# Five edits to a macaron block (mixture of experts, selective scan, mixture of experts) on one core

## The reference

```
def ffn(h):                       # mixture of 8 experts, top 1, and a shared expert
    logits = h @ router_w         # 256 -> 8
    e = argmax(logits); score = sigmoid(max(logits))
    out = silu(xs @ gate_w[e]) * (xs @ up_w[e]) @ down_w[e],  xs = h * score
    return out + silu(h @ sh_gate) * (h @ sh_up) @ sh_down
def ssm(h):                       # selective scan over the 512 tokens, 16 states
    dt_x, B, C = split(h @ W_x.T, [64, 16, 16])
    dt = softplus(dt_x @ W_dt.T + b_dt)
    state = exp(dt * A) * state + dt * B * h
    return sum_n(state * C) + h * D
x = x + 0.5 * ffn(layernorm(x))
x = x + ssm(layernorm(x))
x = x + 0.5 * ffn(layernorm(x))
```

## Time and profile before

| what | us |
|---|---|
| three runs | 507.39, 507.84, 508.14 (median 507.84) |
| the profiled execution, span from first to last instruction | 512.9 |
| busy: PE, DVE, ACT, POOL in that span | 438.5, 342.4, 260.3, 292.6 |

### The profile page before, as it was taken

The page is one execution under the profiler, slowest core; times in us unless marked ns, Lnnn a source line. Parts: engine busy times, 40 slices in busy tenths (PEclk is TensorE's granted clock), DMA queues, the critical chain, the costliest instruction groups (busy, mean ns, idle before and its releaser), DMA issues. The chain is left out here.

```text
span 512.9 us, 7182 instructions
## 1 busy us (share of the span) xinstructions
PE 438.5 (85%) x2264; PEld 309.2 (60%) x2264; DVE 342.4 (67%) x552; ACT 260.3 (51%) x499; POOL 292.6 (57%) x226
## 2 busy tenths in 40 slices
PE   5988899999779597659868886877999999999995
PEld 5855455555334465558767666766984656555553
DVE  5557333333386666988899989999996593333332
ACT  1210233332116669986999999997851111333331
POOL 4302366663324137698799879986891005776463
PEclk9869999999977899989979997998999999999999
DMA  8943122210312012214213331232220298333221
GB/s 286 385 154 92 35 63 65 63 59 32 125 39 64 1 61 65 83 42 105 84 61 97 87 89 63 100 100 69 85 81 1 73 328 280 97 112 103 63 61 39
DMA packets 37667, 49.90 MB, mean 97 GB/s; under 512 B 5498, under 2 KB 26814, under 8 KB 37632
## 3 DMA queue, kind: packets, MB, share of 16 engines
q1 hardware_dynamic: 32368, 38.91, 24.2%
q0 software_dynamic: 5264, 10.54, 7.0%
HBM read 37.33 MB, written 16.70 MB: 105 GB/s over the span
## 5 line engine op out<-in xcount | busy, mean ns | idle before, releaser
L408 POOL TENSOR_TENSOR gs<-hs,c_sb 128x1024 f32<-128x1024 f32 x63 | 148.3, 2370 | 53.0 <-DVE hs L1126 35.5
L1126 DVE TENSOR_TENSOR_SCAN hs<-da,bank 128x1024 f32<-128x1024 f32 x64 | 145.1, 2278 | 9.8 <-PE bank L796 9.7
L796 PE MATMUL bank<-ident,dbx_t 128*128 128x128 f32 x512 | 73.7, 290 | 35.5 <-DVE hs L1126 29.3
L697 PE MATMUL bank<-w_gu,tt 128*128 x184 | 91.1, 617 | 4.1 <-ACT tt L467 4.1
L796 PEld LDWEIGHTS bank<-ident,dbx_t 128*128 128x128 f32 x512 | 60.6, 149 | 50.3 <-DVE hs L1126 39.1
L509 ACT ACTIVATE da<-dt_sb,a_neg 128x511 f32<-128x511 f32 x128 | 84.9, 713 | 7.7 <-DVE hs L1126 7.7
L363 POOL DMA_INDIRECT da<-rows,row_token x46 | 47.2, 1026 | 70.7 <-DVE row_token L1021 57.2
L523 ACT ACTIVATE dbx_t<-dtx_t,h_sb 128x256 f32<-128x256 f32 x194 | 83.8, 497 | 2.7 <-PE bank L796 2.7
L1034 DVE SCALAR_TENSOR_TENSOR q_sb<-th,bank 128x256 f32<-128x256 f32 x46 | 19.4, 421 | 90.2 <-ACT th L462 90.2
L812 PE MATMUL bank<-ident,gs 128*128 128x128 f32 x504 | 71.6, 290 | 8.7 <-POOL gs L408 8.6
L462 ACT ACTIVATE th<-bank,da 128x256 f32<-128x256 f32 x46 | 21.8, 473 | 99.2 <-PE bank L697 99.2
(11 more groups left out here) (125 smaller groups left out, 529.9 us busy)
## 6 DMA issues: line engine op xcount, KB each, us to landing
c_sb<-c_dram SPq DMA_DIRECT2D x64, 256.0 KB, 3.1
rows<-xn_no SPq DMA_DIRECT2D x12, 516.0 KB, 6.5
x_sb<-in_x SPq DMA_DIRECT2D x4, 512.0 KB, 5.8
w_gu<-in_gate_w SPq DMA_DIRECT2D x2, 1024.0 KB, 10.1
w_gu<-in_up_w SPq DMA_DIRECT2D x2, 1024.0 KB, 11.1
w_dn<-in_down_w SPq DMA_DIRECT2D x2, 1024.0 KB, 10.7
xn_no<-token_out SPq DMA_DIRECT2D x4, 512.0 KB, 5.5
rest<-x_sb SPq DMA_DIRECT2D x4, 512.0 KB, 4.9
```

The costliest lines, as they stand in the source:

```text
L408: nc.gpsimd.tensor_tensor(gs[:, s % 2], hs[:, s % RING], c_sb[:, s % RING].unsqueeze(1).to_broadcast([P, KC, L]), ALU.mult).then_inc(sc_g, 1)
L697: last = nc.tensor.matmul(H[j % 2][:, :], tt[:, j % 2, 2 + k], w_gu[:, k, bass.ds(e, 1), :].squeeze(1), start=(k == 0), stop=(k == KC - 1))
L796: mm = nc.tensor.transpose(DBX[s % 2][:, k, i * P:(i + 1) * P], dbx_t[:, s % TURNS, i, k * P:(k + 1) * P], ident[:])
L1126: nc.vector.tensor_tensor_scan(hs[:, s % RING].rearrange(flat), da[:, s % RING].rearrange(flat), DBX[s % 2][:, :, :].rearrange(flat), 0.0, ...
```

## The change

1. **Router in column groups.** w_rt is padded to 32 columns and becomes the stationary operand; the four sequences' 512 tokens stream, and sequence b's logits land in PSUM partitions 32b to 32b+31 of one bank. ACT copies the bank, PE turns it back in four transposes (`route_turn`). The routers leave the scan of the last sequence. Run 0's router moves behind all the layer norm transposes, with both halves of the first shared batch ahead of it.
2. **Reordered transition**, and parts of the lists around it: the shared expert's steps, `normalise(1,1)` behind the softplus, the copies of xnT, `skip` from n=3 to n=6, the memset of the gather slots from between the layer norm's steps to POOL's start.
3. **B's columns behind the transposes**: `project_bt` in the scan comes after `turn_dbx`.
4. **Row table stored once**: one table of rows of 2x258 words; the first seven tiles of run 1 are gathered as half rows, with indices 2t and 2t+1.
5. **Softplus bias in the product**: w_dt has a 65th row, b_dt, and the projection's output has a row of ones there (ACT Identity with a column of the identity matrix as bias). w_x is padded to 128 columns. The relu becomes a max inside a DVE instruction.

```diff
-            def route(r, b):
-                c = 2 * r
-                if r == 1:
-                    pe.wait_ge(sc_dve, states_by("dve", min(N * (BATCH - 1) + (ROUTES + (N,))[b] + 3, STATES)))
-                pe.wait_ge(ln_xnT, (GT // 2) * c + 2 * b + 2)
-                for i in range(LT * b, LT * (b + 1)):
-                    for k in range(KC):
-                        last = nc.tensor.matmul(LG[r][:, i, :], xnT[:, k, i * P:(i + 1) * P], w_rt[:, k, :],
+            def route(r):
+                pe.wait_ge(ln_xnT, (GT // 2) * (2 * r + 1))
+                for k in range(KC):
+                    for b in range(BATCH):
+                        last = nc.tensor.matmul(LG_T[32 * b:32 * (b + 1), :], w_rt[:, k, :], xnT[:, k, b * L:(b + 1) * L],
                                                 start=(k == 0), stop=(k == KC - 1))
+                last.then_inc(rt_lg, 1)
+
+            def route_turn(r):
+                pe.wait_ge(rt_lgc, r + 1)
+                for i in range(LT):
+                    last = nc.tensor.transpose(Y[:, i * P:(i + 1) * P], lg_sb[:, i * P:(i + 1) * P], ident[:])
                 last.then_inc(rt_logits, 1)
...
                 for b in range(BATCH):
-                    sp.dma_start(row_tiles[0][:, rows_of(b), :], xn_no[:, rows_of(b), :]).then_inc(xn_out, 16)
-                for b in range(BATCH if r == 1 else 0):
-                    sp.dma_start(row_tiles[1][:, rows_of(b), 0:D + 2], xn_no[:, rows_of(b), :]).then_inc(rows_full, 16)
+                    sp.dma_start(row_tiles[r][:, rows_of(b), 0:D + 2], xn_no[:, rows_of(b), :]).then_inc(xn_out, 16)
...
             xn_rows(0)
+            sp.wait_ge(ff_out[0], 16 * 2)
+            sp.dma_start(row_tiles[1][:, :, D + 2:], xn_no[:]).then_inc(table_set, 16)
+            sp.wait_ge(table_set, 16)
...
             def project_abs(b, k):
                 act.wait_ge(pj_z, KC * b + k + 1)
-                nc.scalar.activation(w_exp[:, k], pj_bank(b, k), ACT.Abs, bias=b_sb[:, k:k + 1]).then_inc(pj_abs, 1)
-                nc.scalar.activation(dt_sb[:, k, seq(b)], pj_bank(b, k), ACT.Relu, bias=b_sb[:, k:k + 1]).then_inc(pj_max, 1)
+                nc.scalar.activation(w_exp[:, k], pj_bank(b, k), ACT.Abs).then_inc(pj_abs, 1)
+                act.wait_ge(pj_abs, KC * b + k + 1)
+                nc.scalar.activation(w_exp[:, k], w_exp[:, k], ACT.Exp, scale=-1.0).then_inc(pj_exp, 1)
+
+            def project_u(b, k):
+                act.wait_ge(pj_exp, KC * b + k + 1)
+                nc.scalar.activation(dt_sb[:, k, seq(b)], w_exp[:, k], ACT.Copy, bias=1.0).then_inc(pj_u, 1)
...
             def project_w(b, k):
-                nc.vector.tensor_scalar(pj_bank(b, k), w_exp[:, k], 1.0, -1.0, ALU.add, ALU.add).then_inc(pj_w, 1)
-                nc.vector.tensor_tensor(pj_bank(b, k), w_exp[:, k], pj_bank(b, k), ALU.subtract).then_inc(pj_rest, 1)
+                dt = dt_sb[:, k, seq(b)]
+                if b == 0:
+                    nc.vector.tensor_scalar(dt, w_exp[:, k], 1.0, None, ALU.add).then_inc(pj_u, 1)
+                nc.vector.scalar_tensor_tensor(out=dt, in0=dt, scalar=-1.0, in1=w_exp[:, k],
+                                               op0=ALU.add, op1=ALU.subtract).then_inc(pj_rest, 1)
+                nc.vector.scalar_tensor_tensor(out=dt, in0=pj_bank(b, k), scalar=0.0, in1=dt,
+                                               op0=ALU.max, op1=ALU.subtract).then_inc(pj_max, 1)
             def project_dt(b, k):
-                nc.vector.tensor_tensor(pj_bank(b, k), log_w[:, k], pj_bank(b, k), ALU.add).then_inc(pj_sum, 1)
-                nc.vector.tensor_tensor(dt_sb[:, k, seq(b)], pj_bank(b, k), dt_sb[:, k, seq(b)], ALU.add).then_inc(pj_dt, 1)
+                nc.vector.tensor_tensor(dt_sb[:, k, seq(b)], log_w[:, k], dt_sb[:, k, seq(b)],
+                                        ALU.add).then_inc(pj_dt, 1 if b == 0 else KC)
...
             # PE, scan(b), state n
-                    if more and n == 4:
-                        project_bt(b + 1)
-                    if not more and n in ROUTES:
-                        route(1, ROUTES.index(n))
                     if s + 2 < STATES:
                         turn_dbx(s + 2)
+                    if more and n == 4:
+                        project_bt(b + 1)
...
-                    if more and n in (late, late + 1):
-                        project_z(b + 1, n - late)
-                    if n == 3:
+                    for k in range(KC):
+                        if more and n == ((0, 4), (1, 4))[b == 0][k]:
+                            project_z(b + 1, k)
+                    if n == 6:
                         skip(b)
...
             # PE, run 0
-                    shared_gate_up(0, 0, 0)
-                if b > 0:
-                    route(0, b - 1)
-            route(0, BATCH - 1)
+                if b in (1, 2):
+                    shared_gate_up(0, 0, b - 1)
+            route(0)
+            route_turn(0)
+            shared_gate_up(0, 1, 0, (0,))
             count(0)
-            shared_gate_up(0, 0, 1)
-            shared_gate_up(0, 1, 0)
+            shared_gate_up(0, 1, 0, (1,))
             shared_down(0, 0)
+            shared_gate_up(0, 1, 1)
             sequence(0)
-            shared_gate_up(0, 1, 1)
             shared_down(0, 1)
             routed(0)
             for fo in range(KC):
                 shared_gate_up(0, 2, fo)
+            shared_gate_up(0, 3, 0)
             shared_down(0, 2)
...
             project_bt(0)
-            for fo in range(KC):
-                shared_gate_up(0, 3, fo)
-            ln_transposes(1, 2)
+            shared_gate_up(0, 3, 1)
             for h in range(2):
                 turn_dt(0, h)
+            ln_transposes(1, 2)
+            turn_dbx(0)
             ln_transposes(1, 3)
-            turn_dbx(0)
+            turn_dbx(1)
             ln_transposes(1, 4)
-            turn_dbx(1)
             shared_down(0, 3, (0,))
...
             # PE, before run 1
             ln_transposes(2, 7)
+            shared_gate_up(1, 1, 1)
+            route(1)
             shared_down(1, 0, (1,))
-            route(1, BATCH - 1)
-            shared_gate_up(1, 1, 1)
+            route_turn(1)
             count(1)
             shared_gate_up(1, 2, 0)
```

More of the change, by code:

```diff
@@ L182, in macaron_kernel @@
         ln_stats, ln_rstd, ln_xn, ln_tp, ln_xnT = (sem(f"ln_{s}") for s in ("stats", "rstd", "xn", "tp", "xnT"))
-        rt_logits, rt_top, rt_exp, rt_onehot, rt_count, rt_read, rt_expert, rt_score, rt_place, rt_seq, rt_ids = (
-            sem(f"rt_{s}") for s in ("logits", "top", "exp", "onehot", "count", "read", "expert", "score", "place", "seq",
-                                     "ids"))
+        rt_lg, rt_lgc, rt_logits, rt_top, rt_exp, rt_onehot, rt_count, rt_read, rt_expert, rt_score, rt_place, rt_seq, rt_ids = (
+            sem(f"rt_{s}") for s in ("lg", "lgc", "logits", "top", "exp", "onehot", "count", "read", "expert", "score", "place",
+                                     "seq", "ids"))
         sh_gu, sh_tanh, sh_mul, sh_hidden, sh_y, sh_x = (
@@ L200, in macaron_kernel @@
         a_ready = sem("a_ready")
-        pj_all, pj_copy, pj_bt, pj_btc, pj_z, pj_abs, pj_max, pj_exp, pj_w, pj_rest, pj_ln, pj_sum, pj_dt, pj_tp, pj_dtx = (
-            sem(f"pj_{s}") for s in ("all", "copy", "bt", "btc", "z", "abs", "max", "exp", "w", "rest", "ln", "sum", "dt", "tp",
-                                     "dtx"))
+        pj_all, pj_copy, pj_bt, pj_btc, pj_z, pj_abs, pj_exp, pj_u, pj_rest, pj_max, pj_ln, pj_dt, pj_tp, pj_dtx = (
+            sem(f"pj_{s}") for s in ("all", "copy", "bt", "btc", "z", "abs", "exp", "u", "rest", "max", "ln", "dt", "tp", "dtx"))
+        w_pad = sem("w_pad")
         c_rows = sem("c_rows")
@@ L359, in experts, with gather @@
                 rows_back = (token_out, out_flat)[r]
-                def gather(j, lo, hi, source, done):
+                def gather(j, lo, hi, source, done, row):
                     u = j % XR
@@ L374, in experts @@
                 for j in range(XR):
-                    gather(j, 0, WIDE[0], rows[0], ff_in)
+                    gather(j, 0, WIDE[0], (rows[0], half_rows)[r], ff_in, (row_token[:, j:j + 1], row_half[:, 0, j:j + 1])[r])
                 if r == 1:
@@ L386, in experts @@
                     if j + XR < NR:
-                        gather(j + XR, 0, WIDE[r], rows[r], ff_in)
+                        gather(j + XR, 0, WIDE[r], rows[r], ff_in, row_token[:, j + XR:j + XR + 1])
                     if r == 1 and j in DRAINS:
@@ L572, in _ @@
                 project_abs(0, k)
-            project_exp(0)
             project_ln(0)
-            for fo in range(KC):
-                shared_tanh(0, 3, fo)
-            ln_copies(1, 1)
+            shared_tanh(0, 3, 1)
             act.wait_ge(a_ready, 2)
-            ahead(0)
-            ln_copy(1, 4)
+            act.wait_ge(pj_dt, KC)
+            decay(0)
+            ln_copy(1, 2)
+            outer(0)
+            ln_copy(1, 3)
```

(31 more changed lines are left out.)

191 lines of the change are left out of this document (102 added, 89 removed).

## The result

The changed kernel takes 518.75 us (median of 6 runs, 517.09 to 521.19), the kernel before 507.99 (6 runs beside it, 506.08 to 519.68): 1.0223 times as long, 95% interval 1.0188 to 1.0257. The forecast was 495.8, 490 to 504. An execution of the kernel before takes either 501 to 511 us or, with a lower granted clock of TensorE, 514 to 520; the ratios go by the shorter ones alone and the medians by all, and since the one whose rows stand above (span 512.9, clock 0.943) is of the longer kind, a second profile of the same kernel, `before_again` (span 504.6, clock 0.963), is what the changed kernel is measured against here.

A forecast was written before the change was run, and what follows sets the result against it. No single engine bounds the kernel: PE's routed loops and shared expert and DVE's scan follow one another. 4.1 + 7.5 + 1.5 + 2.3 + 1.0 - 4.4 = 12.0 us off 507.84 gives 495.8, range 490 to 504.

The forecast's parts named there:

- Router: Column-group router products on PE: only neighbouring products overlap, because each is a pair of records on the same columns; 3.9 us.
- full overlap: Rival for the router: all four column groups run side by side, 1.7 us, 2.2 better per run, 491.4 in all; chance 0.17.
- Routing of run 0: Way to the first routed tile: earlier rows and shorter router bring it forward; gain 4.1 us, from 2.3 to 5.8.
- The part put down to the memset: Run 0's routing: moving the gather-slot memset off DVE's normalise (4.05 us, elsewhere 1.4) makes the last rows ready 2.7 earlier.
- Transition: Stretch from run 0's routed loop to the scan, reordered; gain 7.5 us, 4 to 10.
- the gain is the clock: Transition: PE idles less, so `project` and `project_z` take 1.7 us each instead of 3.73 and 3.8.
- Scan: The four sequences: gains of 1.5 us in the first, 2.3 in the second and third, 1.0 in the last.
- 8 steps of 0.66 become 4 of 0.7 and one of 1.1: Softplus on DVE in the scan: fewer steps plus a joined addition save 1.4 us a sequence.
- late z less: First scan sequence: one late z fewer, counted within its 1.5 us gain without a size of its own.
- skip and a router leave n=4: Last sequence: without skip (1.8 us) and router (1.7) there, PE starts the next gate and up earlier; gain 1.0 us.
- Way to run 1: Scan's end to run 1's first tile: longer router, four transposes and PE's 1.7 us wait ahead of `count`; loss 4.4, 2.2 to 7.4.
- ACT paces: Rival for the scan: ACT's lead is used up, 2.3 us lost and 0.5 extra paid three times, 499.6; chance 0.09.

The follow-up runs named there:

- before_memset: The kernel before with only GpSimd's memset of the row buffers moved ahead of its rstd work; 506.74 us, ratio 1.002 to the kernel before.
- hidden_first: old_scan with the second gate product of the third shared batch put ahead of combine(0) in VectorE's transition list; 504.72 us, ratio 0.9939 to the kernel before.
- scratch_sbuf: old_scan with the softplus scratch of the second to fourth sequence in SBUF instead of a PSUM bank; 526.1 us, ratio 1.0391 to the kernel before.
- turns_back: skip3 with the turns of dt at steps 8 and 10 again instead of 9 and 11; 509.08 us, ratio 1.0082 to the kernel before.
- skip3: The changed kernel with the skip products at step 3 of each sequence again instead of step 6; 512.93 us, ratio 1.0138 to the kernel before.
- old_scan: The changed kernel with every edit of the scan's lists undone (softplus, skip, B's columns, turns of dt); 505.51 us, ratio 0.9968 to the kernel before.
- best3_warm: old_scan plus hidden_first's exchange, a GpSimd wait, run 1's router earlier, and a last-batch gate and up made twice in the transition; 500.61 us, ratio 0.9913.
- after_warm: The changed kernel with the last shared batch's second-half gate and up products made twice in the transition; 529.18 us, ratio 1.0225 to the kernel before.

## Why the prediction was wrong, step by step

*Router.* 3.9 us forecast, 1.92 measured: the full overlap that was a rival, as the Trainium skill, "TensorEngine Tiling (Array Packing)", Theoretical Speedup, has it with its up to 4x. That pairs of records on the same columns forbid it was wrong.

*Routing of run 0.* 4.1 us earlier forecast, 4.07 against the same profile, 5.7 against before_again. Idle stretch (4.75) and cold down (5.38) came as forecast. The part put down to the memset isn't one by itself (before_memset).

*Transition.* 7.5 us forecast, -0.9 measured (35.62 to 36.54 us from the first gate product to scan 0). The step that failed is "the gain is the clock": 3.73 against 1.7 was read from an execution that fell to half clock there; before_again has 1.96. Against the profile that the forecast was read from, the same stretch is 5.1 us shorter (41.68 to 36.54), inside its 4 to 10. The reordering itself made the transposes late: the down product ahead of them starts 12.4 us behind the first gate product (9.2 in before_again), with a third half ahead of it and its hidden half behind `combine`, and is slow in both (5.4 us); hidden_first gives 2.0 back.

*Scan, the step that decides.* "8 steps of 0.66 become 4 of 0.7 and one of 1.1" and "late z less", 1.5 + 2.3 + 1.0 us to gain; 13.1 lost. (The 1.5 doesn't come out of its terms either: 1.4 less the net 1.2 leaves 0.2, and the late z has no price.) Three things stand in their place. First, three of the new form's five steps work in SBUF alone, where GpSimd's products block them: 2.35 instead of 1.1 and 0.91 instead of 0.69; scratch_sbuf shows the mechanism by itself. VectorE's busy time in the first three sequences, forecast 4.2 lower, is 1.1 higher. Second, moved steps wait for other engines: 3.4 for u at n=3, of which the forecast had seen 1.2, and 5.2 for the turn of dt at n=11, whose queue neighbour, the addition, was not followed to GpSimd's normalise (turns_back takes these waits away and is 2.8 us shorter by the ratios). VectorE's idle time in the first three sequences grows by 7.6. Third, "skip and a router leave n=4" was counted as a gain; without them a second GpSimd product stands beside VectorE's normalise, and skip at 6 meets TensorE at half clock (0.50): 4.4 us in the last sequence (skip3). The parts overlap: undone alone, softplus gives 9.3 and skip 4.3 by the ratios, together with B's columns 12.9. The softplus's part is by the windows more waits than form, but no run takes the form back alone; turns_back to old_scan, some 1.1% by their ratios, is the form, its places and B's columns.

*Way to run 1.* -4.4 forecast with a router of 3.9, so -2.4 with the measured one; -2.6 measured. Right, and PE's wait ahead of `count` is the 1.7 forecast, answering:
```profile
402.66 1.92 PE L647 MATMUL bank<-xnT,w_rt 128*32 128x512 f32 x16
...
408.62 0.23 PE L660 MATMUL bank<-onehot,before 128*128 128x128 bf16 x1 [1.68 <-DVE onehot L986]
```

*ACT paces, memory, routed loops.* Not seen: ACT is busy 184.0 us of the scan, 183.0 before, and the loops moved by 0.5 and 0.4 us.

The sum was also carried from one long execution to a median of short ones unscaled. The range left 0.07 for the other side and described it by the router's clock alone; no case had the scan's engines blocking each other, though one row of a VectorE step at 4.05 us beside a GpSimd memset was on the table.

## What to carry to other kernels

When a VectorE step is rewritten, count where its operands lie: moving a scratch from PSUM to SBUF next to a busy GpSimd cost 21 us for 24 steps (scratch_sbuf). A step that is moved on a full engine is followed through the queue that feeds it, two engines far; and an edit that removes work may free a neighbour to collide. Take a second profile of the same kernel before pricing a stretch at half clock.

## What the runs showed of the hardware

Four column groups of 32 ran side by side in float32: 16 records of 512 columns in 1.92 us where 4 alone took 1.98. A VectorE float32 step of 128x512 with one SBUF input and an SBUF result took 0.40 to 0.42 us, with a PSUM result 0.67. With two SBUF inputs it took 0.69, and beside a GpSimd product of 2.37 us up to 2.75; the scan, with one input in PSUM, took 2.25 to 2.29 in all 64 states of before_again, changed, old_scan and scratch_sbuf. Four products (eight records) made twice, with no other use than to keep TensorE busy for 3.4 us, went with 2.75 us less in best3_warm and with no change that could be told in after_warm.
